# Fused attention and LoRA feed-forward layer: token stores moved from SyncE's queue to ScalarE's, and the order of two value products swapped in stage 1

## The chip, the cores and the metric

The kernel runs on one core of a Trainium2 chip. The metric is device time in microseconds of one execution. TensorE (PE) does matmuls and transposes, VectorE (DVE), ScalarE (ACT) and GpSimd (POOL) work on tiles in SBUF and PSUM, and SyncE (SP) issues most DMAs. Each engine runs its own instruction list strictly in order, and the lists meet at semaphores.

## The reference

Input x has 2 x 1024 tokens of 512 values. After a layernorm, two branches are computed on the same normalised tokens and added to x:

```python
xn = layernorm(x)
Q, K, V = heads(xn @ wq.T + bq), heads(xn @ wk.T + bk), heads(xn @ wv.T + bv)   # 16 heads of 32
Q, K = elu(Q) + 1, elu(K) + 1
KV = sum over tokens of K^T V;  K_sum = sum over tokens of K
att = (Q @ KV) / (Q . K_sum + 1e-8) @ wo.T + bo
scores = sigmoid(xn @ W_router); the best 2 of 8 experts by scores + expert_bias, weights w
gate = xn @ W_gate + shared LoRA + sum over experts of w * LoRA_e   (rank 8, scale 1/8)
up   = the same with W_up
ffn  = hidden @ W_down + LoRAs,  hidden = silu(gate) * up           (1376 wide)
out = x + att + ffn
```

## The kernel before, in words

All products are done as three matmuls on values split into a high part (fp32r) and the rest: high x high, high x low, low x high (`product`, L1216 to L1221). So each input needs a rounding on ScalarE (`round_to`, seen in the trace as L667) and a subtraction on VectorE (`sub`, seen as L865).

Stage 1 walks over 16 tiles of 128 tokens. Each engine has its own `stage1(t, half, s)`, called by `tiles` (L367): tiles 0 and 1 unrolled, 2 to 7 in a loop of pairs, 8 to 15 unrolled. s is the parity of t and picks one of two slots of most buffers. The order of the work is written out by hand in each list. For tile t, TensorE (L1260 to L1280) does:

1. K(t): keys, 12 matmuls of 512 columns into bank 1 (in the trace bank<-wk_h,xt and bank<-wk_l,xt);
2. T(t+1): four transposes of the next tile's normalised tokens xn (L1236);
3. on even tiles from 2 on, KV: 64 small matmuls that sum keys by values of the two tiles before (L1248);
4. Va(t): the first 384 value columns, 12 matmuls (128x384 in the trace), into ps_va;
5. Vz(t): the last 128 value columns with the 152 columns of LoRA and router, 12 matmuls (128x280), into ps_vz;
6. L(t-2): two transposes (L1257) of the LoRA values of tile t-2, weighted by their experts (the tile zst).

Tile 0 has T(1) between Va and Vz instead of behind K.

VectorE in tile t (L933 to L972): kb (L937, the keys plus bias, after K(t)), `compare(t-1)` of the router, the low part of the tokens of t+1 (`tokens_lo`, tile xt), `lora_weighted(t-2)` (L916 and L920, which write zst and release L(t-2)), layernorm statistics of t+2, `select(t-1)`, kf (L952), xn of t+2 (L878, after GpSimd's rstd), zraw (L960, a copy of Vz's last 152 columns), on even tiles `key_values` (L890), in tiles 8 to 11 the low part of a quarter of wq and in tiles 12 to 15 of wo, and `lora_lo(t-2)` (L929 and L930, tile zt, after ScalarE's high part).

ScalarE in tile t (L681 to L703): `tokens_hi(t+1)` (the high part of xt; it waits until the store of tile t-1, which used the same slot, has landed), krelu, kexp, the values of Va into vf (va_done), in tiles 8 to 15 a quarter of wq or wo (`WQ_PART`, `WO_PART`), then after zraw the values of Vz into vf (vf_done), rexp (L701), and `lora_out(t-2)` (the high part of zt, which waits for L(t-2)).

GpSimd computes rstd and the router's ranks and weights (`route`, L595). The split tokens xt of each tile go to the DRAM scratch scr_x by one DMA of 512 KB a tile, issued by SyncE (L430 to L432) behind the load of x for tile t+3 (L428); stage 2 (attention output) and stage 3 (feed-forward) read them back. Around these SyncE also issues stores of zt (L421), reads of scr_x (L411, L415) and the loads of down and up weights (L448, L445). After tile 0's store it issues some 3 MB of constants and weights (L437 to L442).

After tile 15 TensorE goes on with transposes of the summed keys by values (L1299) and the first queries, and from about a third of the span on the program is the feed-forward stage alone.

In the prediction and the rows, kb(t) is the instruction L937 of tile t, and K(t), T(t), Va(t), Vz(t), L(t), KV are the products above.

Of the kernel before, what the change touches and what calls it, by code (L numbers as in the profile page):

```python
# [19 lines left out]
ACT = mybir.ActivationFunctionType  # L20
F32 = mybir.dt.float32
F32R = mybir.dt.float32r

P = 128
BATCH, SEQ, D = 2, 1024, 512
TOK = BATCH * SEQ
KD = D // P
TILES = TOK // P
# [5 lines left out]
HEADS, DK = 16, 32  # L34
HC = P // DK
LO = DK // 2
E, R = 8, 8
# [4 lines left out]
NZ = 2 * ER + 2 * R + E  # L42
NV = D + NZ
VA = 3 * P
# [28 lines left out]
def program(nc, dram, out, scr_x, scr_z, scr_att, scr_w):  # L73
    ctx = ExitStack()
    with ctx:
        def sem(name):
            return ctx.enter_context(nc.semaphore(name))
# [20 lines left out]
        def at(name, shape, dt=F32):  # L98

            size = 4 * math.prod(shape[1:])  # L100
            t = nc.alloc_sbuf_tensor_at(name, shape, dt, offset=place[0])
            place[0] += -(-size // 32) * 32
            assert place[0] <= nc.sbuf_usable_end, (name, place[0])
            return t
# [57 lines left out]
        va_h = at("va_h", [P, KD, NV], F32R)  # L162
        va_l = at("va_l", [P, KD, NV], F32R)
# [3 lines left out]
        xt = at("xt", [P, 2, 2, KD, P], F32R)  # L167
# [9 lines left out]
        vf = at("vf", [P, 2, KD, HC, AUG])  # L177
# [16 lines left out]
        zraw = at("zraw", [P, 2, NZ])  # L194
        rexp = at("rexp", [P, E])
# [46 lines left out]
        ps_va, ps_vz = bank[4][:, 0:VA], bank[5][:, 0:P + NZ]  # L242
# [14 lines left out]
        wsetl_done = sem("wsetl_done")  # L257
# [6 lines left out]
        xtl_done = sem("xtl_done")  # L264
# [4 lines left out]
        va_ready = sem("va_ready")  # L269
        va_done = sem("va_done")  # L270
        vf_done = sem("vf_done")
        vz_ready = sem("vz_ready")
        zraw_done = sem("zraw_done")
        rexp_done = sem("rexp_done")
# [6 lines left out]
        scr_xd = [sem("scr_x_even"), sem("scr_x_odd")]  # L281
# [80 lines left out]
        def wait(eng, s, value):  # L362

            if not isinstance(value, int) or value > 0:
                eng.wait_ge(s, value)
# [11 lines left out]
        def behind(t, n):  # L377

            return not isinstance(t, int) or t >= n

        def ahead(t, n):

            return not isinstance(t, int) or t + n < TILES
# [11 lines left out]
        def _(sp):  # L395
            def load_x(t, s):
                sp.dma_start(xin[:, s, :], dram["x"][bass.ds(t * P, P), :]).then_inc(xin_in[s], 16)
# [16 lines left out]
            def x3_load(g):  # L414
                sp.dma_start(x3[:].rearrange("p t i k n -> p t (i k n)").bitcast(F32), scr_x[:, bass.ds(g * GT, GT)]  # L415
                             ).then_inc(x3_in, 16)
# [7 lines left out]
            def stage1(t, s, more=True):  # L424
                if more:

                    sp.wait_ge(ln_done, t + 2)
                    load_x(t + 3, 1 - s)  # L428

                sp.wait_ge(xtl_done, t + 1)  # L430
                sp.dma_start(scr_x[:, bass.ds(t, 1)], xt[:, s:s + 1].rearrange("p o i k n -> p o (i k n)").bitcast(F32)
                             ).then_inc(scr_xd[s], 16)  # L432

            stage1(0, 0)

            for dst, name in ((hmask, "headmask"), (hcol, "headcol"), (hrow_raw, "headrow"), (lomask, "lomask"), (bdn_raw, "b_dn"), (sb_dn, "sb_dn")):
# [49 lines left out]
            def x3r_load(t, s):  # L486
                sp.dma_start(x3r[:, s, :], dram["x"][bass.ds(t * P, P), :]).then_inc(x3r_in[s], 16)
# [20 lines left out]
            for j in range(2, GT):  # L508
                x3r_load(j, j)
            sp.wait_ge(q_ready, KD * 2)  # L510
            x3_load(2)
            sp.wait_ge(m_ready, BATCH * KD)
            for c in range(WO_CHUNK, X3_CHUNK):
# [151 lines left out]
        def _(act):  # L665
            def round_to(dst, src):
                return nc.scalar.activation(dst, src, ACT.Copy)  # L667
# [6 lines left out]
            def lora_out(t):  # L674
# [3 lines left out]
                round_to(zt4[:, :, 1], pst)  # L678
                round_to(zt4[0:ER, :, 0], pst[0:ER]).then_inc(zhi_done, 1)

            def stage1(t, half, s):  # L681
                first = isinstance(t, int) and t == 0
                if ahead(t, 1):
                    tokens_hi(t + 1, 1 - s, half + s)
                act.wait_ge(kb_done, t + 1)
                nc.scalar.activation(krelu[:], kb[:], ACT.Relu, scale=-1.0).then_inc(krelu_done, 1)
                act.wait_ge(krelu_done, t + 1)
                wait(act, kf_done, t)
                nc.scalar.activation(kexp[:], krelu[:], ACT.Exp, scale=-1.0).then_inc(kexp_done, 1)
                act.wait_ge(va_ready, t + 1)  # L690
                round_to(vf[:, s, 0:KD - 1, :, 0:DK], ps_va.rearrange("p (k h n) -> p k h n", h=HC, n=DK)).then_inc(va_done, 1)
                if isinstance(t, int) and t in WQ_PART:

                    act.wait_ge(s2_in, 16 * STAGE2_LOADS)
                    round_to(wq_h[:, WQ_PART[t]], w_raw[:, 1, WQ_PART[t]]).then_inc(wqh_done, 1)
                if isinstance(t, int) and t in WO_PART:
                    round_to(wo_h[:, WO_PART[t]], w_raw[:, 0, WO_PART[t]]).then_inc(woh_done, 1)

                act.wait_ge(zraw_done, t + 1)
                round_to(vf[:, s, KD - 1, :, 0:DK], ps_vz[:, 0:P].rearrange("p (h n) -> p h n", n=DK)).then_inc(vf_done, 1)  # L700
                nc.scalar.activation(rexp[:], zraw[:, s, NZ - E:], ACT.Exp, scale=-1.0).then_inc(rexp_done, 1)  # L701
                if behind(t, 2):
                    lora_out(t - 2)  # L703

# [510 lines left out]
        def _(pe):  # L1215
# [7 lines left out]
            def tile_of(dst, s, wh, wl, split_before=None):  # L1223

                for k in range(KD):
                    if split_before is not None:
                        pe.wait_ge(wsetl_done, split_before + k + 1)
                    last = product(dst, (xt_h[:, s, k, :], xt_l[:, s, k, :]), (wh[:, k, :], wl[:, k, :]),
                                   k == 0, k == KD - 1)
                return last  # L1230

            def transpose_tokens(t):
                pe.wait_ge(ln_done, t + 1)
                wait(pe, xtl_done, t)
                for k in range(KD):
                    last = nc.tensor.transpose(ps_xt[:, k * P:(k + 1) * P], xn[:, k * P:(k + 1) * P], ident[:])  # L1236
                last.then_inc(xt_ready, 1)

            def keys_by_values(t, pair, s):

                pe.wait_ge(kf_done, t + 1)
                pe.wait_ge(vf_done, t + 1)
                if s == 0:
                    pe.wait_ge(kvacc_done, pair + 1)
                for c in range(KD):
                    for h in range(HC):
                        col = c * P + h * DK
                        last = nc.tensor.matmul(ps_kv[h * DK:(h + 1) * DK, c * AUG:(c + 1) * AUG],  # L1248
                                                kf[:, s, col:col + DK], vf[:, s, c, h, :],
                                                start=(s == 0 and c == 0), stop=(s == 1), skip_group_check=True)  # L1250
                last.then_inc(kv_ready, 1)

            def lora_transposed(t):
                pe.wait_ge(zst_done, t + 1)
                wait(pe, zt_done, t)
                for k in range(2):
                    last = nc.tensor.transpose(ps_zt[:, k * P:(k + 1) * P], zst[:, k, :], ident[:])  # L1257
                last.then_inc(zt_ready, 1)

            def stage1(t, half, s):  # L1260
                first = isinstance(t, int) and t == 0
                pe.wait_ge(xtl_done, t + 1)
                wait(pe, kb_done, t)
                tile_of(ps_k[:], s, wk_h, wk_l, split_before=0 if first else None).then_inc(k_ready, 1)
                if ahead(t, 1) and not first:
                    transpose_tokens(t + 1)
                if s == 0 and behind(t, 2):
                    keys_by_values(t - 2, half - 1, 0)
                    keys_by_values(t - 1, half - 1, 1)
                wait(pe, va_done, t)  # L1270
                tile_of(ps_va, s, va_h[:, :, 0:VA], va_l[:, :, 0:VA], split_before=KD if first else None
                        ).then_inc(va_ready, 1)
                if first:
                    transpose_tokens(1)
                wait(pe, vf_done, t)
                if first:
                    pe.wait_ge(wsetl_done, 2 * KD + 1)
                tile_of(ps_vz, s, va_h[:, :, VA:], va_l[:, :, VA:]).then_inc(vz_ready, 1)
                if behind(t, 2):
                    lora_transposed(t - 2)  # L1280

            pe.sem_inc(u_ready, 1)
            pe.sem_inc(d_done, 1)
# [105 lines left out]
            kv_transposed(1)  # L1389
            queries(0, (3,))  # L1390
            pe.wait_ge(vf_done, TILES)
            pe.wait_ge(zraw_done, TILES)
            pe.wait_ge(zt_done, TILES - 1)
            m_of(0)
# [203 lines left out]
```

## Time and profile before

| What | us |
|---|---|
| Median of 3 runs | 674.25 (672.67 to 675.02) |
| Profiled execution, its time | 671.93 |
| Its span, first to last instruction | 670.1 |
| PE busy | 660.1 (99%) |
| DVE busy | 375.5 (56%) |
| ACT busy | 256.2 (38%) |
| POOL busy | 126.5 (19%) |

The granted TensorE clock is full over the whole span. Busy time is the union of an engine's instructions; the ends of matmuls are modelled and each overlaps the next, so the distance between the starts of two matmuls tells more of PE's pace than the duration of one. In the timeline each row has the start in us, the duration in us, the engine, the line, the operation, output<-input, and in brackets the time that the engine had been idle before it and what released it.

### The profile page before, as it was taken

How to read it: one execution, taken by the hardware profiler on the slowest of the kernel's cores; microseconds unless marked ns; L12 is line 12 of the kernel's file. 1: busy time of each engine (PE TensorE's matmuls, PEld its weight loads, DVE VectorE, ACT ScalarE, POOL GpSimd, SP SyncE). 2: the span in 40 equal slices, each digit the busy share in tenths (PEclk: the TensorE clock that was granted, in tenths of full speed). 3: DMA queues.
4: the chain of work that ended last, by engine and by line, in shares of the span. 5: the costliest groups of instructions: out<-in, count | busy, mean ns of one | idle time of the engine just before them, and what ended most of it. 6: DMA issues, size and time to landing. Idle time of an engine off the chain costs nothing.

```text
span 670.1 us, 10338 instructions
## 1 busy us (share of the span) xinstructions
PE 660.1 (99%) x3568; PEld 545.6 (81%) x3568; DVE 375.5 (56%) x697; ACT 256.2 (38%) x412; POOL 126.5 (19%) x290
## 2 busy tenths in 40 slices
PE   7999999999999999999999999999999999999998
PEld 6888999977777788888888888888888888888886
DVE  5577888778775956334345443445444326534433
ACT  4334454467235423323233333243233324323321
POOL 3466666636246230000000000000000000000000
PEclk9999999999999999999999999999999999999999
DMA  8856566754844679950025100011500001300001
GB/s 258 297 182 202 193 214 204 256 222 163 307 183 153 235 225 3 9 195 0 1 78 201 51 0 0 0 67 75 188 0 0 0 3 75 126 0 0 0 0 63
DMA packets 40778, 74.21 MB, mean 111 GB/s; under 512 B 19296, under 2 KB 20192, under 8 KB 38832
## 3 DMA queue, kind: packets, MB, share of 16 engines
q1 hardware_dynamic: 40400, 73.43, 39.0%
q0 software_dynamic: 208, 0.30, 0.4%
q8 instruction: 16, 0.26, 0.2%
q10 hardware_dynamic: 144, 0.13, 0.1%
q14 instruction: 10, 0.08, 0.0%
HBM read 52.81 MB, written 21.04 MB: 110 GB/s over the span
## 4 chain that ended last, share of the span: by engine, by line
PE 74%; POOL 9%; issue 6%; DVE 4%; DMA 2%; ACT 2%; POOLq 1%; SPq 0%; DVEq 0%; ACTq 0%
PE bank L1461 18%; PE bank L1219 15%; PE bank L1220 15%; PE bank L1221 15%; PE bank L1434 6%; DVE den L1065 2%; PE bank L1447 1%; PE bank L1445 1%; POOL vare L578 1%; POOL rstd L580 1%; POOL gt L605 1%; DMA scr_z<-zt 1%; POOL ssum L616 1%; DMA w_raw<-in_wkT 1%; POOL ssum L612 1%
## 5 line engine op out<-in xcount | busy, mean ns | idle before, releaser
L1219 PE MATMUL bank<-x,up_h 128*128 128x512 f32 (+1 forms) x352 | 137.1, 390 | 0.2 <-DVE x3r L1030 0.2
L1220 PE MATMUL bank<-x,up_h 128*128 128x512 f32 (+1 forms) x352 | 137.0, 389 | 0.0
L1221 PE MATMUL bank<-x,up_l 128*128 128x512 f32 (+1 forms) x352 | 136.9, 389 | 0.0
L1156 DVE TENSOR_TENSOR hf<-bank,silu 128x512 f32<-128x512 f32 x44 | 30.4, 692 | 154.5 <-issue 134.8
L1461 PE MATMUL bank<-dn,hid_h 128*128 128x512 f32 x352 | 108.8, 390 | 0.0
L667 ACT ACTIVATE hid_h<-hf 128x512 fp32r<-128x512 f32 x44 | 27.8, 633 | 142.5 <-DVE hf L1156 142.5
L1219 PEld LDWEIGHTS bank<-x,up_h 128*128 128x128 f32 x352 | 66.1, 188 | 14.4 <-issue 0.7
L1461 PEld LDWEIGHTS bank<-dn,hid_h 128*128 128x128 f32 x352 | 65.9, 188 | 14.5 <-DVE res L1181 0.6
L1221 PEld LDWEIGHTS bank<-x,up_l 128*128 128x128 f32 x352 | 66.1, 188 | 13.8
L1220 PEld LDWEIGHTS bank<-x,up_h 128*128 128x128 f32 x352 | 66.1, 188 | 13.6
L865 DVE TENSOR_TENSOR up_l<-up_raw,up_h 128x1024 fp32r<-128x1024 f32 x44 | 55.0, 1250 | 26.9 <-ACT up_h L667 26.9
L1461 PE MATMUL bank<-dn,hid_l 128*128 128x512 f32 x176 | 68.5, 389 | 0.0
L667 ACT ACTIVATE up_h<-up_raw 128x1536 fp32r (+1 forms) x44 | 64.6, 1474 | 1.7 <-DVE qf_odd L1023 1.7
L824 ACT ACTIVATE silu<-bank 128x512 f32<-128x512 f32 x44 | 26.3, 597 | 100.3 <-PE bank L1434 100.3
L1434 PE MATMUL bank<-z,up_h 128*128 128x512 f32 x176 | 54.2, 389 | 0.0
L865 DVE TENSOR_TENSOR hid_l<-hf,hid_h 128x512 fp32r<-128x512 f32 x44 | 30.5, 692 | 35.5 <-ACT hid_h L667 35.5
L667 ACT ACTIVATE dn<-dn_raw 128x576 fp32r (+1 forms) x44 | 30.1, 684 | 33.3 <-PE bank L1447 22.3
L1219 PE MATMUL bank<-va_h,xt 128*128 128x384 f32 (+1 forms) x128 | 41.9, 327 | 0.8 <-DVE va_l L865 0.8
L1221 PE MATMUL bank<-va_h,xt 128*128 128x384 f32 (+1 forms) x128 | 40.3, 315 | 0.0
L1220 PE MATMUL bank<-va_l,xt 128*128 128x384 f32 (+1 forms) x128 | 40.2, 314 | 0.0
L865 DVE TENSOR_TENSOR up_h<-up_raw,up_h 64x256 fp32r<-64x256 f32 x88 | 38.6, 439 | 0.6
L1461 PEld LDWEIGHTS bank<-dn,hid_l 128*128 128x128 f32 x176 | 33.0, 188 | 6.9
(166 smaller groups left out, 1081.0 us busy)
## 6 DMA issues: line engine op xcount, KB each, us to landing
x<-scr_x SPq DMA_DIRECT2D x7, 2048.0 KB, 7.5
up_raw<-in_ffn_up SPq DMA_DIRECT2D x11, 768.0 KB, 7.9
scr_x<-xt SPq DMA_DIRECT2D x16, 512.0 KB, 5.3
xin<-in_x SPq DMA_DIRECT2D x16, 256.0 KB, 4.5
scr_z<-zt SPq DMA_DIRECT2D x16, 256.0 KB, 2.0
x3r<-in_x SPq DMA_DIRECT2D x16, 256.0 KB, 3.6
scr_att<-x3r SPq DMA_DIRECT2D x16, 256.0 KB, 2.2
z<-scr_z SPq DMA_DIRECT2D x4, 1024.0 KB, 5.0
```

The source lines that it names most:

```text
L578: nc.gpsimd.tensor_tensor(vare[:], mv[:, 1:2], epsln[:], ALU.add).then_inc(vare_done, 1)
L580: nc.gpsimd.tensor_tensor(rstd[:], vare[:], mhalf[:], ALU.pow).then_inc(ln_rstd, 1)
L667: return nc.scalar.activation(dst, src, ACT.Copy)
L824: nc.scalar.activation(silu[:], ps_g[:], ACT.Silu).then_inc(silu_done, 1)
L865: return nc.vector.tensor_tensor(dst, a, b.bitcast(F32), ALU.subtract)
L1065: nc.vector.reciprocal(den[:], den[:]).then_inc(rden_done, 1)
L1156: nc.vector.tensor_tensor(hf[:], ps_u[:], silu[:], ALU.mult).then_inc(h_done, 1)
L1219: nc.tensor.matmul(dst, lh, rh, start=start, stop=False, **kw)
L1220: nc.tensor.matmul(dst, lh, rl, start=False, stop=False, **kw)
L1221: return nc.tensor.matmul(dst, ll, rh, start=False, stop=stop, **kw)
L1434: last = nc.tensor.matmul(dst[:], up_h[:, s, col:col + P], z4[:, :, a * 2 + b, :], start=False, stop=(b == 1))
L1461: d = nc.tensor.matmul(ps_out[j][:], h[:, s, cols], w[:, s, 0:DNB - 1], start=(first and i == 0), stop=False, skip_group_check=True)
```

## The change

Token stores: SyncE no longer issues them. ScalarE issues the store of tile t+1 in its tile t behind kexp, after a wait for the low part of the tokens of t+1; in tile 0 it issues those of tile 0 and 1. SyncE waits for all 16 stores before it reads back the third group of tokens.

Order in tiles 1 to 15: TensorE does Vz(t), then L(t-2), then Va(t). ScalarE evacuates Vz and does rexp first, then the part of wq or wo, then the values of Va, then `lora_out(t-2)`. Tile 0 keeps its order. VectorE's and GpSimd's lists are unchanged. KV waits for va_done of both tiles, since it is now the later one.

```diff
 # SyncE, stage1
-                sp.wait_ge(xtl_done, t + 1)
-                sp.dma_start(scr_x[:, bass.ds(t, 1)], xt[:, s:s + 1]...).then_inc(scr_xd[s], 16)
 # SyncE, stage 2
             sp.wait_ge(q_ready, KD * 2)
+            for s in range(2):
+                sp.wait_ge(scr_xd[s], 16 * TILES // 2)
             x3_load(2)
 # ScalarE
+            def store_tokens(t, s):
+                act.wait_ge(xtl_done, t + 1)
+                act.dma_start(scr_x[:, bass.ds(t, 1)], xt[:, s:s + 1]...).then_inc(scr_xd[s], 16)
 # ScalarE, stage1, behind kexp
-                act.wait_ge(va_ready, t + 1)
-                round_to(vf[:, s, 0:KD - 1, :, 0:DK], ps_va...).then_inc(va_done, 1)
+                if first:
+                    store_tokens(0, 0)
+                if ahead(t, 1):
+                    store_tokens(t + 1, 1 - s)
+                def values_out():
+                    act.wait_ge(va_ready, t + 1)
+                    round_to(vf[:, s, 0:KD - 1, :, 0:DK], ps_va...).then_inc(va_done, 1)
+                if first:
+                    values_out()
+                act.wait_ge(zraw_done, t + 1)
+                round_to(vf[:, s, KD - 1, :, 0:DK], ps_vz[:, 0:P]...).then_inc(vf_done, 1)
+                nc.scalar.activation(rexp[:], zraw[:, s, NZ - E:], ACT.Exp, scale=-1.0).then_inc(rexp_done, 1)
                 if isinstance(t, int) and t in WQ_PART:
                     act.wait_ge(s2_in, 16 * STAGE2_LOADS)
                     round_to(wq_h[:, WQ_PART[t]], w_raw[:, 1, WQ_PART[t]]).then_inc(wqh_done, 1)
                 if isinstance(t, int) and t in WO_PART:
                     round_to(wo_h[:, WO_PART[t]], w_raw[:, 0, WO_PART[t]]).then_inc(woh_done, 1)
-                act.wait_ge(zraw_done, t + 1)
-                round_to(vf[:, s, KD - 1, :, 0:DK], ...).then_inc(vf_done, 1)
-                nc.scalar.activation(rexp[:], ...).then_inc(rexp_done, 1)
+                if not first:
+                    values_out()
                 if behind(t, 2):
                     lora_out(t - 2)
 # TensorE, keys_by_values
                 pe.wait_ge(vf_done, t + 1)
+                pe.wait_ge(va_done, t + 1)
 # TensorE, stage1: values_a() is Va(t); values_z() is Vz(t), then L(t-2)
+                if first:
+                    values_a()
                     transpose_tokens(1)
+                    values_z()
+                else:
+                    values_z()
+                    values_a()
 # TensorE, ahead of m_of(0)
             pe.wait_ge(vf_done, TILES)
+            pe.wait_ge(va_done, TILES)
```

## Rows read from the trace of the kernel before

**Rows 1.** Busy time by stretch: us, then each engine's busy us, PEclk, DMA.

```profile
32.00:34.00 2.00, 1.18 (x8) 0.87 (x7) 1.90 (x9) 1.55 (x4) 0.00 (x0) 1.00 0.09 35
...
60.00:80.00 20.00, 20.00 (x231) 18.50 (x218) 15.56 (x52) 8.82 (x21) 11.65 (x39) 1.00 0.62 202
...
140.00:160.00 20.00, 19.36 (x92) 14.64 (x92) 15.98 (x25) 14.94 (x29) 4.54 (x5) 1.00 0.42 160
```

**Rows 2.** Timeline of PE, tile 7 into tile 8, from T(8) to T(9).

```profile
67.17 0.60 PE L1236 MATMUL bank<-ident_sb,xn 128*128 128x128 f32 x4
...
67.53 0.42 PE L1219 MATMUL bank<-va_h,xt 128*128 128x384 f32 x1
...
69.71 0.29 PE L1219 MATMUL bank<-va_h,xt 128*128 128x280 f32 x1
...
71.25 0.38 PE L1257 MATMUL bank<-ident_sb,zst 128*128 128x128 f32 x2
71.39 0.48 PE L1219 MATMUL bank<-wk_h,xt 128*128 128x512 f32 x1
...
74.28 0.60 PE L1236 MATMUL bank<-ident_sb,xn 128*128 128x128 f32 x4
```

**Rows 3.** Timeline of DVE, tile 7 and the start of tile 8.

```profile
68.22 0.69 DVE L937 TENSOR_TENSOR kb<-bank,bk_b 128x512 f32<-128x512 f32 x1
...
70.38 0.35 DVE L920 TENSOR_TENSOR zst<-zraw,wtok 128x64 f32<-128x64 f32 x2
...
73.39 0.31 DVE L960 COPY zraw<-bank 128x152 f32<-128x152 f32 x1
...
74.67 0.42 DVE L865 TENSOR_TENSOR zt<-bank,zt 64x256 fp32r<-64x256 f32 x1 [0.97 <-ACT zt L667]
...
75.62 0.69 DVE L937 TENSOR_TENSOR kb<-bank,bk_b 128x512 f32<-128x512 f32 x1
```

**Rows 4.** Timeline of ACT, tile 7 behind zraw.

```profile
73.74 0.28 ACT L667 ACTIVATE vf<-bank 128x128 f32<-128x128 f32 x1 [3.11 <-DVE zraw L960]
...
74.01 0.63 ACT L667 ACTIVATE zt<-bank 128x256 fp32r<-128x256 f32 x2
```

**Rows 5.** Timeline of DVE and ACT, tile 9 (with a part of wq).

```profile
83.25 0.69 DVE L937 TENSOR_TENSOR kb<-bank,bk_b 128x512 f32<-128x512 f32 x1
...
85.18 0.47 ACT L667 ACTIVATE vf<-bank 128x384 f32<-128x384 f32 x1
...
85.55 0.62 ACT L667 ACTIVATE wq_h<-w_raw 128x512 fp32r<-128x512 f32 x1
...
90.66 0.69 DVE L937 TENSOR_TENSOR kb<-bank,bk_b 128x512 f32<-128x512 f32 x1
```

**Rows 6.** Timeline of PE and DVE, tile 2: T(3), kb(2), L(0).

```profile
27.21 0.60 PE L1236 MATMUL bank<-ident_sb,xn 128*128 128x128 f32 x4
27.51 0.69 DVE L937 TENSOR_TENSOR kb<-bank,bk_b 128x512 f32<-128x512 f32 x1 [1.84 <-PE bank L1221]
...
33.16 0.44 PE L1257 MATMUL bank<-ident_sb,zst 128*128 128x128 f32 x2 [0.82 <-DVE zst L920]
```

**Rows 7.** ACT around the stores of tiles 0 and 1, and ScalarE's one DMA.

```profile
17.23 0.63 ACT L689 ACTIVATE kexp<-krelu 128x512 f32<-128x512 f32 x1
...
20.98 0.60 ACT L667 ACTIVATE xt<-bank 128x512 fp32r<-128x512 f32 x1 [0.29 <-PE bank L1236]
...
667.86 0.38 ACTq L389 DMA_DIRECT2D out<-res  x1
```

**Rows 8.** DMA issues of the page: KB each, median us to landing.

```profile
scr_x<-xt SPq DMA_DIRECT2D x16, 512.0 KB, 5.3
```

**Rows 9.** Waits over the span, us in total, times, longest us.

```profile
ACT xt L667 <- DMA scr_x<-xt: 13.4, 5, 5.3
```

**Rows 10.** Timeline, tile 15: kb(15), and PE's first transposes behind stage 1.

```profile
128.20 0.69 DVE L937 TENSOR_TENSOR kb<-bank,bk_b 128x512 f32<-128x512 f32 x1
...
131.43 0.60 PE L1299 MATMUL bank<-ident_sb,kvm 128*128 128x128 f32 x4
```

More of the change, by code:

```diff
@@ L428, in stage1 @@
                     load_x(t + 3, 1 - s)
-                sp.wait_ge(xtl_done, t + 1)
-                sp.dma_start(scr_x[:, bass.ds(t, 1)], xt[:, s:s + 1].rearrange("p o i k n -> p o (i k n)").bitcast(F32)
-                             ).then_inc(scr_xd[s], 16)
             stage1(0, 0)
@@ L679, in lora_out @@
                 round_to(zt4[0:ER, :, 0], pst[0:ER]).then_inc(zhi_done, 1)
+            def store_tokens(t, s):
+                act.wait_ge(xtl_done, t + 1)
+                act.dma_start(scr_x[:, bass.ds(t, 1)], xt[:, s:s + 1].rearrange("p o i k n -> p o (i k n)").bitcast(F32)
+                              ).then_inc(scr_xd[s], 16)
             def stage1(t, half, s):
@@ L689, in stage1 @@
                 nc.scalar.activation(kexp[:], krelu[:], ACT.Exp, scale=-1.0).then_inc(kexp_done, 1)
-                act.wait_ge(va_ready, t + 1)
-                round_to(vf[:, s, 0:KD - 1, :, 0:DK], ps_va.rearrange("p (k h n) -> p k h n", h=HC, n=DK)).then_inc(va_done, 1)
+                if first:
[4 more added lines that the diff above has]
+                    act.wait_ge(va_ready, t + 1)
+                    round_to(vf[:, s, 0:KD - 1, :, 0:DK], ps_va.rearrange("p (k h n) -> p k h n", h=HC, n=DK)).then_inc(va_done, 1)
+                if first:
+                    values_out()
+                act.wait_ge(zraw_done, t + 1)
+                round_to(vf[:, s, KD - 1, :, 0:DK], ps_vz[:, 0:P].rearrange("p (h n) -> p h n", n=DK)).then_inc(vf_done, 1)
+                nc.scalar.activation(rexp[:], zraw[:, s, NZ - E:], ACT.Exp, scale=-1.0).then_inc(rexp_done, 1)
                 if isinstance(t, int) and t in WQ_PART:
@@ L697, in stage1 @@
                     round_to(wo_h[:, WO_PART[t]], w_raw[:, 0, WO_PART[t]]).then_inc(woh_done, 1)
-                act.wait_ge(zraw_done, t + 1)
-                round_to(vf[:, s, KD - 1, :, 0:DK], ps_vz[:, 0:P].rearrange("p (h n) -> p h n", n=DK)).then_inc(vf_done, 1)
-                nc.scalar.activation(rexp[:], zraw[:, s, NZ - E:], ACT.Exp, scale=-1.0).then_inc(rexp_done, 1)
+                if not first:
+                    values_out()
                 if behind(t, 2):
@@ L1269, in stage1, with values_a, values_z @@
                     keys_by_values(t - 1, half - 1, 1)
-                wait(pe, va_done, t)
-                tile_of(ps_va, s, va_h[:, :, 0:VA], va_l[:, :, 0:VA], split_before=KD if first else None
-                        ).then_inc(va_ready, 1)
+                def values_a():
+                    wait(pe, va_done, t)
+                    tile_of(ps_va, s, va_h[:, :, 0:VA], va_l[:, :, 0:VA], split_before=KD if first else None
+                            ).then_inc(va_ready, 1)
+                def values_z():
+                    wait(pe, vf_done, t)
+                    if first:
+                        pe.wait_ge(wsetl_done, 2 * KD + 1)
+                    tile_of(ps_vz, s, va_h[:, :, VA:], va_l[:, :, VA:]).then_inc(vz_ready, 1)
+                    if behind(t, 2):
+                        lora_transposed(t - 2)
                 if first:
+                    values_a()
                     transpose_tokens(1)
[L1275 to L1280, printed above, removed]
+                    values_z()
+                else:
+                    values_z()
+                    values_a()
             pe.sem_inc(u_ready, 1)
```

## The prediction

> **What bounds the kernel now.** I read the busy time by stretch first: in stage 1 PE is busy 20.00 of 20 us while DVE has 15.56 and ACT 8.82 [rows 1]. PE's timeline says the same more sharply. T(8) to T(9) is 7.11 us with no idle bracket: T 0.36, Va 2.18, Vz 1.54, L 0.14, K 2.89 [rows 2]. So steady stage 1 is TensorE's stream and nothing in it waits. What waits is little: L(0) came 0.82 us late, for zst [rows 6], behind a token store that ScalarE waited 5.3 us for [rows 9]. Then I read DVE, which never waits for PE in this stretch: kb(7) to kb(8) is 7.40 us [rows 3], paced by its own list and by ACT's high part of zt, which it waited 0.97 us for. DVE is nearly as full a loop as PE, and that is what the change has to be read against.
>
> **What the early Vz can release: nothing.** Vz(7) starts at 69.71 and L(5) behind it at 71.25 [rows 2], but zraw(7) starts at 73.39 [rows 3], 2.1 us after. zraw is held by its place in DVE's list, which is unchanged. Making Vz end 2.18 us earlier brings zraw, rexp and the router not one step forward.
>
> **What the order adds on TensorE.** L(t-2) moves ahead of Va(t). It needs zst, which DVE finishes at kb(t) + 2.51: 68.22 to 70.38 + 0.35 [rows 3]. kb(t) itself waits for K(t): at T(3) 27.21 it started at 27.51, 0.30 later [rows 6]. So L can go no earlier than T + 0.30 + 2.51 + 0.04, where 0.04 is a handover (zraw's end 73.70, ACT's next at 73.74) [rows 3, 4]. That is T + 2.85. On odd tiles PE is there at T + 0.36 + 1.54 = T + 1.90, so it stands idle 0.95. On even tiles KV fills the gap. Before, Va lay between and hid it: L(5) at T + 4.08 was 0.5 behind zst's end at 70.73 [rows 2, 3]. The new loop of a tile is K end, kb, zst, L, Va, K: 0.30 + 2.51 + 0.04 + 0.14 + 2.18 + 2.89 = 8.06 us, odd or even. It closes on itself, so lateness isn't made up.
>
> **What the order adds on ScalarE.** Behind zraw stand vf of Vz, rexp and the high part of zt, at 73.74 and 74.01 [rows 4], and DVE waits for the last before kb(t+1). The change puts the values of Va in between: 0.37, the distance from that instruction to the next (85.18 to 85.55) [rows 5]. DVE's loop becomes 7.40 + 0.37 = 7.77, still under 8.06. In tiles 8 to 15 the part of wq or wo (0.62) also moves from the idle time ahead of zraw to behind rexp. I take 0.52 for it, its duration less the 0.10 by which the instruction ahead of it overlaps its start [rows 5]. DVE's low part of wq or wo waits for it too, but ends before zt's high part does. Loop: 7.41 (kb(9) to kb(10)) + 0.37 + 0.52 = 8.30 [rows 5], which is over 8.06 and so sets the pace there. Bounds: 8.06, if the part is hidden after all, and 7.41 + 0.47 + 0.62 = 8.50.
>
> **The stores.** SP loses 16 issues; nothing waits for them there but the loads behind. ScalarE gains 16 issues; its one such row is 0.38 us [rows 7]. From tile 1 on each lies behind kexp, in the idle time before vf, 3.11 us in tile 7 [rows 4]: nothing. Without that cover it would be 15 x 0.38 = 5.7. The waits for landed stores (13.4 us on ACT in all [rows 9]) go, since a store now starts some tile earlier than it is needed, but only the first ever reached PE. The start pays something: store 0 can't be issued before kexp(0) ends at 17.86, and lands by the median 5.3 [rows 7, 8] at 23.2, where ACT took xt(2) at 20.98. With 0.60 and about 0.69 for the two halves of xt, K(2) may start at 24.5; before, it started near 27.21 - 2.89 = 24.3 [rows 2, 6]. With kb and kf behind it I take 0.3. Bounds: 0, if it lands by 21, and 3.3, if it waits the 5.3 us that a store cost before [rows 9]: 5.3 less the 2.0 between xt(2)'s end and K(2). All of SP's constants and weights travel in that time. The Trainium skill ("DMA: Bandwidth & Descriptors", Queues, rings and completion order) says that each DMA engine goes round the queues that have work, a packet from each. By this rule a store on ScalarE's queue passes SP's backlog instead of standing in it, and the start costs the 0.3 or less; its section on issuing engines says that they share the same 16 engines, which speaks for more. No row of before has bulk on both queues.
>
> **Sum, as positions.** T(3) at 27.21 + 0.3 = 27.5. Six tiles at 8.06 put T(9) at 75.9; it was 74.28 [rows 2]. The stall of tile 2 is won and lost again in there. kb(8) is at 76.2, seven loops at 8.30 (tile 14 has head sums in place of statistics, taken as equal) put kb(15) at 134.3, against 128.20 [rows 10]: 6.1 late. Tile 15 has no tokens to round, so zst comes at kb + 2.51 - 0.60 (an estimate from the 0.6 that ACT's like instruction takes), then 0.04, L 0.14, Va 2.18: PE enters stage 2 at kb + 4.27 = 138.6, where it was 131.43 [rows 10], 7.1 late. DVE and ACT are only 6.1 late there, and PE had 0.64 idle in the stretch behind [rows 1], so some 0.6 comes back. The rest of the program is a full PE stream and moves by the same 6.5. From 671.93 of the profiled execution that is 678.4. The median of the runs is 2.3 above that execution, so the forecast is **680.7**.
>
> By bounds: the second pace at 8.06 takes 1.7 off, at 8.50 adds 1.4; the start takes 0.3 off or adds 3.0; the return may be 0 or 1.5. That is 677.8 to 685.7, the ends hardly together.
>
> **Rivals.**
> - *Faster.* zst comes in time for the moved L. The point is T + 1.90 on odd tiles, and it needs kb or the router's steps on DVE 0.95 earlier than rows show. If so, PE keeps its stream. T(3) to T(9) took 47.07 us [rows 2, 6] where the six tiles from kb(9) to kb(15) took 44.95 [rows 5, 10]; those 2.1 go with the store's wait, the 0.64 of stage 2 with them, and it ends at 671.5. Against it: DVE's list is the same and kb can't precede K's end. Chance 0.06.
> - *No difference.* The waits exist but overlap: DVE's loop stays near 7.5, PE loses 0.3 or so on odd tiles only, about 2 us, which eats the 2.1 won at the start: 674.2. Chance 0.06.
> - *Late stores.* The forecast, and store 0 lands as late as store 1 did: 683.7. For it, the backlog of weights; against it, the queue of its own. Chance 0.08.
> - *The clock.* The granted clock is 1.00, the 2.4 GHz level, even where PE was busy 1.18 of 2.00 us [rows 1], so idle times of 1 us in 8 shouldn't move it. At 1.2 GHz each tile's 7.11 us of PE work would double: three tiles make 21 us, so about 702. Chance 0.02. The Trainium skill ("TensorE: Matmul & The Clock Gate", A second HAM failure mode) describes small idles between groups of matmuls that make the clock swing; so far the trace speaks against it here.
>
> **How the numbers follow.** The forecast has 0.78. About 0.3% (2 us) is what a measurement of this kernel can tell from no change. Slower: 0.78 + 0.08 + 0.02 = 0.88; same 0.06; faster 0.06. The range takes the forecast's bounds and the late stores, and leaves out the other three: 677.0 to 685.5.
>
> **What would show it.** Right: an idle bracket of about 0.9 at L1257 released by zst L920 on odd tiles, T to T near 8.1 in tiles 3 to 7; kb to kb near 8.3 in tiles 8 to 13 with DVE waiting 1 us and more for zt; kb released by PE in tiles 3 to 7; PE busy some 6 us less than its span grows to; no wait of ACT for scr_x beyond tile 2. The store step is wrong if xt(2) on ACT starts after 24. The whole is wrong if T to T over tiles 9 to 14 stays near 7.5: then zst doesn't hang on kb as I read it.

## The result and the profile after

The changed kernel takes 682.74 us (median of 5 runs, 682.11 to 684.03) against 673.47 us before. The ratio is 1.0137, interval 1.0123 to 1.0151: slower by 9.3 us. The profiled execution took 683.07 us, span 681.3.

The page's first part and the busy time by stretch show where: PE does the same work and is no longer full in stage 1 (from 60 to 80 us it was busy 20.00 of 20 us before, [rows 1], and 19.39 after).

```profile
PE 662.3 (97%) x3568; PEld 545.4 (80%) x3568; DVE 376.1 (55%) x697; ACT 255.6 (38%) x412; POOL 124.3 (18%) x290
...
40.00:60.00 20.00, 17.92 (x166) 16.05 (x166) 15.22 (x52) 7.75 (x19) 11.20 (x36) 1.00 0.63 192
60.00:80.00 20.00, 19.39 (x170) 17.15 (x169) 13.13 (x42) 7.33 (x21) 12.16 (x40) 1.00 0.67 223
...
100.00:120.00 20.00, 18.94 (x166) 16.77 (x166) 14.58 (x45) 8.59 (x23) 12.41 (x38) 1.00 0.53 186
```

The timeline of tile 7 answers to [rows 2] and [rows 3]: T(8), kb(7), zst, L(5), Va(7), then T(9).

```profile
71.90 0.60 PE L1248 MATMUL bank<-ident_sb,xn 128*128 128x128 f32 x4
72.10 0.69 DVE L949 TENSOR_TENSOR kb<-bank,bk_b 128x512 f32<-128x512 f32 x1
...
74.26 0.35 DVE L932 TENSOR_TENSOR zst<-zraw,wtok 128x64 f32<-128x64 f32 x2
...
74.66 0.44 PE L1270 MATMUL bank<-ident_sb,zst 128*128 128x128 f32 x2 [0.61 <-DVE zst L932]
74.86 0.42 PE L1231 MATMUL bank<-va_h,xt 128*128 128x384 f32 x1
...
79.83 0.60 PE L1248 MATMUL bank<-ident_sb,xn 128*128 128x128 f32 x4
80.03 0.69 DVE L949 TENSOR_TENSOR kb<-bank,bk_b 128x512 f32<-128x512 f32 x1 [0.20 <-PE bank L1233]
```

L now waits for zst, which VectorE finishes 2.51 us after kb (74.61). T to T is 7.93 us where it was 7.11, and kb(8) is released by PE, which never happened there before. The even tile in front of it, where KV fills the gap, hardly changed: T(7) to T(8) is 8.03 us where it was 7.99. Over a pair of tiles the pace went from 7.55 to 7.98 a tile. The idle bracket, 0.61, is smaller than the loss of 0.8, because the modelled end of the last matmul before it reaches into the gap.

The timeline of tile 9 answers to [rows 4, 5]. Behind zraw stand vf of Vz, the part of wq, the values of Va and zt:

```profile
88.34 0.69 DVE L949 TENSOR_TENSOR kb<-bank,bk_b 128x512 f32<-128x512 f32 x1
...
93.50 0.31 DVE L972 COPY zraw<-bank 128x152 f32<-128x152 f32 x1
93.84 0.28 ACT L665 ACTIVATE vf<-bank 128x128 f32<-128x128 f32 x1 [3.48 <-DVE zraw L972]
...
94.12 0.62 ACT L665 ACTIVATE wq_h<-w_raw 128x512 fp32r<-128x512 f32 x1
94.64 0.48 ACT L665 ACTIVATE vf<-bank 128x384 f32<-128x384 f32 x1
94.77 0.69 DVE L877 TENSOR_TENSOR wq_l<-w_raw,wq_h 128x512 fp32r<-128x512 f32 x1 [0.96 <-ACT wq_h L665]
95.01 0.64 ACT L665 ACTIVATE zt<-bank 128x256 fp32r<-128x256 f32 x2
95.68 0.42 DVE L877 TENSOR_TENSOR zt<-bank,zt 64x256 fp32r<-64x256 f32 x1 [0.21 <-ACT zt L665]
...
96.63 0.69 DVE L949 TENSOR_TENSOR kb<-bank,bk_b 128x512 f32<-128x512 f32 x1
```

The distances are 0.52 for the part and 0.37 for the values, and kb to kb is 8.29 where it was 7.41. VectorE's wait shows at the low part of wq (0.96) more than at zt.

**Where the 11.1 us between the two profiled executions lie**, from the starts of T, kb and the first transposes behind stage 1 in both timelines:

| Stretch | before | after | difference |
|---|---|---|---|
| start to T(1) | 15.45 | 17.32 | +1.87 |
| T(1) to T(3) | 11.76 | 12.75 | +0.99 |
| T(3) to T(5), tiles 2 and 3 | 16.88 | 17.83 | +0.95 |
| T(5) to T(9), tiles 4 to 7 | 30.19 | 31.93 | +1.74 |
| T(9) to T(15), tiles 8 to 13 | 45.30 | 49.42 | +4.12 |
| T(15) to L1299 (L1321 after) | 11.85 | 13.37 | +1.52 |
| from there to the end | 538.67 | 538.68 | 0.0 |

All that the change takes away before T(1) is the issue of store 0, at 13.96 in the kernel before, and nothing waits for that store there. Over all the experiments below T(1) starts between 15.70 and 18.64, the latest of them with store 0 on SyncE, so I put its 1.87 down to the single execution; 11.1 - 1.9 = 9.2 is then near the 9.3 of the medians.

### The profile page after: what moved, and what is told of

It is laid out like the page before. It is cut to its first block, busy times and chain, and to the rows that moved or that the text cites. A ratio compares the mean times of both kernels' runs of the same rounds, so it can differ in the third digit from the quotient of the medians.

```text
span 681.3 us, 10343 instructions
## 1 busy us (share of the span) xinstructions
PE 662.3 (97%) x3568; PEld 545.4 (80%) x3568; DVE 376.1 (55%) x697; ACT 255.6 (38%) x412; POOL 124.3 (18%) x290
## 4 chain that ended last, share of the span: by engine, by line
PE 77%; POOL 9%; issue 7%; DVE 4%; DMA 2%; ACT 1%; POOLq 1%; SPq 0%; DVEq 0%; ACTq 0%
PE bank L1484 17%; PE bank L1231 16%; PE bank L1232 16%; PE bank L1233 16%; PE bank L1457 6%; DMA w_raw<-in_wvT 2%; PE bank L1470 1%; PE bank L1468 1%; POOL vare L576 1%; POOL gt L603 1%; POOL rstd L578 1%; DVE den L1077 1%; POOL ssum L614 1%; POOL ssum L610 1%; POOL gt L601 1%
## 5 line engine op out<-in xcount | busy, mean ns | idle before, releaser
L1231 PE MATMUL bank<-va_h,xt 128*128 128x384 f32 (+1 forms) x128 | 43.2, 337 | 1.1 <-DVE va_l L877 1.1
L1233 PE MATMUL bank<-va_h,xt 128*128 128x384 f32 (+1 forms) x128 | 40.4, 316 | 0.0
```

The source lines that it names most:

```text
L1231: nc.tensor.matmul(dst, lh, rh, start=start, stop=False, **kw)
L1233: return nc.tensor.matmul(dst, ll, rh, start=False, stop=stop, **kw)
```

## The experiments

Each was run beside the kernel before, in 5 to 12 executions, and its ratio is to the kernel before of the same rounds. Pace means T to T or kb to kb, from the timeline.

**Order alone and stores alone.**

```diff
 # e1_order_alone: the changed kernel, SyncE's stage1 as before
+                sp.wait_ge(xtl_done, t + 1)
+                sp.dma_start(scr_x[:, bass.ds(t, 1)], ...)
 # ScalarE
-                if first:
-                    store_tokens(0, 0)
-                if ahead(t, 1):
-                    store_tokens(t + 1, 1 - s)
 # e2_stores_alone: the kernel before, with store_tokens behind kexp on ScalarE, none on SyncE
```

> Edit: the stores are issued by SyncE again, the new order of TensorE and ScalarE stays. Theory (two loops, one over TensorE's wait for zst, one over ScalarE's work behind zraw, make the slowdown): 682 to 685 us, ratio to before 1.012 to 1.017; the start is about 1 us cheaper than after, ScalarE's waits for landed stores on even tiles come back and may add some tenths a tile. Rival (stores on ScalarE's queue cost most of it): 673 to 676.

> Edit: the kernel before, with only the token stores moved to ScalarE. Theory: T(3) about 1 us later than before for store 0, ScalarE's other waits for landed stores gone, TensorE's stream else unchanged: 672.5 to 675, ratio 0.998 to 1.002. Rival (the stores cost): 679 or more, kb to kb over 7.6 in tiles 8 to 13.

Measured: order alone 684.43 us, ratio 1.0155 (1.0137 to 1.0173); stores alone 672.95 us, ratio 0.9987 (0.9978 to 0.9996). The slowdown is the order's. In order alone the pace was 7.98 in tiles 5 and 6 and 8.28 in tiles 9 to 12, as after; the tenths that I had feared from the landed stores on even tiles didn't come, since the longer tile gives them time. Its start was dearer than after, not cheaper: ScalarE waited 5.39 us for store 1 and L(0) came 3.34 us late, because in this order L(0) stands ahead of Va(2) with nothing to hide behind. Behind this idle time the granted clock was at 0.50, the 1.2 GHz level, from 34.25 to 40.75, and T(3) to T(4) took 14.27 us (9.05 after). A stretch of it:

```profile
36.00:40.00 4.00, 4.00 (x13) 3.90 (x13) 1.30 (x4) 0.89 (x4) 3.01 (x10) 0.50 0.02 4
```

6.5 us at the half level are some 3.3 us of PE's work lost, an estimate. Only this execution of order alone has a trace. It is the slowest of five, with a mean granted clock of 0.993; the fastest, 682.83, has 1.000. So part of the difference between order alone and the changed kernel can be the clock's.

**Which loop costs what.** Four kernels put back one piece or two of the order.

```diff
 # e3_L_behind_Va: the changed kernel, TensorE
                 else:
                     values_z()          # without lora_transposed
                     values_a()
+                if behind(t, 2):
+                    lora_transposed(t - 2)
 # e4_parts_early: the changed kernel, ScalarE: the WQ_PART and WO_PART blocks ahead of
 #   act.wait_ge(zraw_done, t + 1)
 # e5_parts_and_zt_early: as e4, and
-                if not first:
-                    values_out()
                 if behind(t, 2):
                     lora_out(t - 2)
+                if not first:
+                    values_out()
 # e6_L_behind_Va_ACT_short: e3 and e5 together
```

> Edit: the changed kernel with L(t-2) behind Va(t) again, Vz(t) still first, ScalarE's new order kept. Theory: TensorE's wait for zst at L is gone, but DVE's loop over ScalarE stays: kb to kb 7.8 in tiles 4 to 7 (8.0 in the changed kernel), 8.3 in tiles 8 to 13 as in the changed kernel, TensorE's idle time moves to K(t) or KV; 680 to 682, ratio 1.009 to 1.013. Rival (the place of L is the whole cost): 673 to 675.

> Edit: the changed kernel with ScalarE's part of wq or wo ahead of the wait for zraw, as before. Theory: DVE's loop is 7.8 and TensorE's loop over zst, 8.0, sets the pace in all tiles: T to T 8.0 in tiles 9 to 14 (8.28 in the changed kernel), 6 to 7 tiles x 0.28 = 1.8 us off: 680.5 to 681.5. Rival (only DVE's loop counts, the wait for zst is a symptom): pace 7.8, 679.

> Edit: as e4, and the high part of zt ahead of the values of Va. ScalarE's order behind zraw is then as short as before, L(t-2) is still ahead of Va(t). Theory: TensorE's loop over zst stays, pace 8.0 as in e4, 680 to 681.5, idle brackets at L on odd tiles. Rival (ScalarE's order is the whole cost): 673 to 675.

> Edit: the changed kernel with L(t-2) behind Va(t) and ScalarE's part of wq or wo ahead of the wait for zraw, the high part of zt ahead of the values of Va; only the swap of Va and Vz and the stores stay. Theory: both loops are back at 7.4 or less, TensorE streams, T to T 7.55 in tiles 9 to 14: as e2, 672.5 to 675. Rival (the swap of Va and Vz itself costs): 678 or more.

| Kernel | us | ratio to before | pace, tiles 5 and 6 | pace, tiles 9 to 12 |
|---|---|---|---|---|
| after | 682.74 | 1.0137 (1.0123 to 1.0151) | 7.98 | 8.28 |
| L behind Va | 679.83 | 1.0097 (1.0079 to 1.0115) | 7.82 | 8.30 |
| parts early | 680.52 | 1.0123 (1.0101 to 1.0145) | 7.98 | 7.97 |
| parts and zt early | 680.14 | 1.0104 (1.0087 to 1.0121) | 7.98 | 7.98 |
| all three | 673.06 | 1.0013 (0.9986 to 1.0040) | 7.54 | 7.55 |

(Paces of T in all but L behind Va, where they are of kb.) The ratios are the ones to compare: the kernel before had a median of 673.59 beside the first and the last of the four experiments and of 672.77 beside the other two. Each loop alone holds the kernel at 680, and only without both is TensorE's stream back at the 7.55 of before. The medians hide two of the eleven executions of the last kernel, which took 679.97 and 680.38 us with mean granted clocks of 0.995 and 0.990; the other nine lie between 671.71 and 673.55. These two have no trace, and what held them stays open. With ScalarE's list as short as before, PE still waits for zst and still releases kb. PE and DVE in the kernel with parts and zt early, from T(10) to T(11) and kb(10):

```profile
87.42 0.60 PE L1248 MATMUL bank<-ident_sb,xn 128*128 128x128 f32 x4
87.62 0.69 DVE L949 TENSOR_TENSOR kb<-bank,bk_b 128x512 f32<-128x512 f32 x1 [0.61 <-PE bank L1233]
...
90.18 0.44 PE L1270 MATMUL bank<-ident_sb,zst 128*128 128x128 f32 x2 [0.61 <-DVE zst L932]
...
95.34 0.60 PE L1248 MATMUL bank<-ident_sb,xn 128*128 128x128 f32 x4
95.55 0.69 DVE L949 TENSOR_TENSOR kb<-bank,bk_b 128x512 f32<-128x512 f32 x1 [0.56 <-PE bank L1233]
```

With L behind Va, kb(10) stands 2.68 us behind T(11), far from K's end; that loop runs over VectorE and ScalarE, without PE:

```profile
91.74 0.60 PE L1248 MATMUL bank<-ident_sb,xn 128*128 128x128 f32 x4
...
94.42 0.69 DVE L949 TENSOR_TENSOR kb<-bank,bk_b 128x512 f32<-128x512 f32 x1
```

**TensorE's loop, shortened from another side.** If it runs over zst, an earlier zst must shorten it by as much.

```diff
 # e12_zst_early: as parts and zt early; VectorE, stage1
+                if behind(t, 2):
+                    lora_weighted(t - 2, s)
                 if ahead(t, 1):
                     tokens_lo(t + 1, 1 - s)
-                if behind(t, 2):
-                    lora_weighted(t - 2, s)
```

> Edit: as e5 (the changed order on TensorE, ScalarE's list as short as before), and VectorE weights the LoRA values of t-2 before it takes the low part of the tokens of t+1, so zst is ready some 0.6 us earlier. Theory (TensorE's loop runs over kb, zst, L, Va, K): the loop falls from 7.97 to about 7.4, which only odd tiles (7.11 of TensorE's own work) still feel; two tiles take 15.3 to 15.5 us against 15.94 in e5 and 15.10 before, the idle time at L on odd tiles falls from 0.6 to 0.2 or less: 675 to 677. Rival (something else than zst's place paces e5): 680.

Measured: 675.68 us, ratio 1.0035 (1.0022 to 1.0048). T(7) to T(9) took 15.31 us and T(9) to T(11) 15.29, where the kernel it was made from has 15.97 and 15.90, and from tile 4 to tile 14 no bracket stands at L any more. T(9), L(7) in tile 9 and T(11):

```profile
76.58 0.60 PE L1248 MATMUL bank<-ident_sb,xn 128*128 128x128 f32 x4
...
86.70 0.44 PE L1270 MATMUL bank<-ident_sb,zst 128*128 128x128 f32 x2
...
91.87 0.60 PE L1248 MATMUL bank<-ident_sb,xn 128*128 128x128 f32 x4
```

Shortened by some 0.6, the loop of 7.98 should be 7.4, over the 7.11 of TensorE's own work on odd tiles and under its 7.99 on even ones: odd tiles took 7.3 us and even ones 7.98. The loop over zst is shown by its size, not only by its presence.

**The start.** Store 0 back on SyncE, in the old order and in the new.

```diff
 # e7_store0_on_SP (from stores alone), e8_after_store0_on_SP (from the changed kernel)
 # SyncE
             stage1(0, 0)
+            sp.wait_ge(xtl_done, 1)
+            sp.dma_start(scr_x[:, 0:1], xt[:, 0:1]...).then_inc(scr_xd[0], 16)
 # ScalarE, behind kexp
-                if first:
-                    store_tokens(0, 0)
```

> Edit: as e2 (old order, stores on ScalarE), but store 0 is issued by SyncE where it was before. Theory: K(2) isn't late any more, the wait of 5.3 us for store 1 on SyncE's queue is gone, so T(3) to T(4) falls from 9.0 towards 8.0: 671.5 to 673, ratio 0.996 to 0.999. Rival (store 1 lands as late on its own queue, the weights take the bandwidth): as before, 673 to 674.

> Edit: the changed kernel, but store 0 is issued by SyncE where it was before. Theory: ACT takes xt(2) without a wait for the store, K(2) not 0.8 late, 0.8 to 1.5 us off the changed kernel: 681 to 682. Rival (the start's delay is hidden behind L(0)'s wait): 682.7.

Both missed. In the old order 673.15 us, ratio 1.0002 (0.9992 to 1.0013): nothing won. In the new order 684.30 us, ratio 1.0174 (1.0150 to 1.0197), no better than after and probably worse, since the two intervals barely touch. The rival of the first had the number, 673 to 674, but not the cause, for store 1 wasn't late: it landed 6.7 us after its issue. The rival of the second, 682.7, missed too. The wait for store 0 did go, and T(1) to T(3) in the new order fell from 12.75 to 11.79. But VectorE's statistics of tile 4 then waited for x, 3.10 us in the first and 2.51 in the second. Timeline of DVE and PE in the first of the two:

```profile
35.02 0.69 DVE L877 BATCH_NORM_STATS2 stats<-xin 128x6 f32<-128x512 f32 x1 [3.10 <-DMA xin<-in_x]
...
37.90 0.66 PE L1244 MATMUL bank<-ident_sb,xn 128*128 128x128 f32 x4 [0.64 <-DVE xn L886]
```

In the new order this delay went on into PE: L(1) came 2.75 us late, and behind that idle time the granted clock was at 0.50 from 42.75 to 45.75. A stretch of it:

```profile
43.00:45.00 2.00, 2.00 (x8) 2.00 (x7) 1.26 (x5) 0.00 (x0) 1.63 (x5) 0.50 0.85 264
```

In the kernel after, the wait for x is there too, 0.87, behind 3.14 for store 0 and 0.82 for L(0):

```profile
25.70 0.60 ACT L665 ACTIVATE xt<-bank 128x512 fp32r<-128x512 f32 x1 [3.14 <-DMA scr_x<-xt]
...
27.17 0.50 PE L1231 MATMUL bank<-wk_h,xt 128*128 128x512 f32 x1 [0.68 <-DVE xt L877]
...
30.79 0.60 ACT L665 ACTIVATE xt<-bank 128x512 fp32r<-128x512 f32 x1
...
33.96 0.44 PE L1270 MATMUL bank<-ident_sb,zst 128*128 128x128 f32 x2 [0.82 <-DVE zst L932]
...
34.77 0.69 DVE L881 BATCH_NORM_STATS2 stats<-xin 128x6 f32<-128x512 f32 x1 [0.87 <-DMA xin<-in_x]
```

xt(3) (30.79) has no wait for store 1, which in the kernel before cost 5.3 us there. In the first of the two experiments store 1, alone on ScalarE's queue, landed 6.7 us after its issue, where on SyncE's queue, behind 2 MB of wo and wq, it took 10.9: it passes the backlog. In the kernel after it stands behind store 0 and took 9.8 us, and it comes in time mostly because it is issued 2.3 us behind T(1) and not 5.0. The load of x for tile 4 stays behind the weights: issued at 21.96, landed near 34.7. It stood behind them in the kernel before as well, issued at 20.09 and landed 10.0 us later, but there VectorE was held until 32.05 by the wait for store 1 and found x ready. The next kernels test that.

```diff
 # e9 (from e7), e10 (from the kernel before), e11 (from e8): SyncE
-            sp.wait_ge(wsetl_done, 2 * KD)
-            sp.dma_start(w_raw[:, 0], dram["woT"]).then_inc(s2_in, 16)
-            sp.dma_start(w_raw[:, 1], dram["wqT"]).then_inc(s2_in, 16)
             ...
             stage1(1, 1)
+            sp.wait_ge(wsetl_done, 2 * KD)
+            sp.dma_start(w_raw[:, 0], dram["woT"]).then_inc(s2_in, 16)
+            sp.dma_start(w_raw[:, 1], dram["wqT"]).then_inc(s2_in, 16)
```

> Edit: as e7 (old order, stores on ScalarE, store 0 on SyncE), and SyncE issues its loads of wo and wq (1 MB each) behind the load of x for tile 4. Theory (the 2 MB of weights hold up whatever stands behind them on SyncE's queue: store 1 in the kernel before, x of tile 4 with the stores moved): DVE's wait for x of tile 4 (3.1 us in e7) is gone, T(3) to T(4) falls from 8.8 to 8.0 or less, T(4) to T(5) to 7.1 to 7.5; 1.3 to 2 us off before: 671 to 672, ratio 0.997 to 0.998. Rival (bandwidth, not order, holds them up): as e7, 673.

> Edit: the kernel before, with only the loads of wo and wq moved behind the load of x for tile 4 and store 1 on SyncE. Theory: store 1 lands by the 5 us of others, ScalarE's wait of 5.3 us before xt(3) is gone, as e9: 671 to 672, ratio 0.997 to 0.998; the queue that carries the stores makes no difference. Rival (ScalarE's queue is what frees store 1): 673.5, as before.

> Edit: the changed kernel, with store 0 on SyncE and the loads of wo and wq behind the load of x for tile 4. Theory: the whole start of the change's cost (T(1) to T(5), 30.6 us in the changed kernel against 28.6 before) goes, the loops stay at 7.97 and 8.29: 680.5 to 682. Rival (the start is noise of the single profile): 682.7 to 684.

Measured: 671.92 us, ratio 0.9975 (0.9965 to 0.9984); 671.12 us, ratio 0.9968 (0.9955 to 0.9980); 679.27 us, ratio 1.0089 (1.0076 to 1.0102), a little better than I had allowed. In the second, the old kernel with nothing but the weights moved, ScalarE takes xt(3) right behind its transposes, the statistics don't wait, and T(3) to T(4) is 8.01 us (9.03 before). The weights are issued only 0.5 us behind store 1, so the same bytes travel, yet store 1 landed 6.4 us after its issue (10.9 before) and x of tile 4 5.7 (10.0 before):

```profile
27.75 0.60 PE L1236 MATMUL bank<-ident_sb,xn 128*128 128x128 f32 x4
28.48 0.60 ACT L667 ACTIVATE xt<-bank 128x512 fp32r<-128x512 f32 x1 [1.87 <-PE bank L1236]
...
30.49 0.68 DVE L869 BATCH_NORM_STATS2 stats<-xin 128x6 f32<-128x512 f32 x1
...
35.76 0.60 PE L1236 MATMUL bank<-ident_sb,xn 128*128 128x128 f32 x4
```

With the weights out of the way it makes no clear difference which queue carries the stores (the two intervals overlap), and both versions beat both kernels. So it is the place in the queue that delayed the start; the bytes are the same, and the weights are only asked for from tile 8 on. And the order of the change alone, with a clean start on either side, costs 1.0089 - 0.9975 = 1.1%, or 7.7 us (7.4 by the medians). The stretches from T(5) on in the table above add up to the same, 1.74 + 4.12 + 1.52 = 7.4.

## Why the prediction was right, and where its sizes were off

**Direction and mechanism: right.** The range held the time, and both loops are there as built. Over the kernel before the forecast was +6.5 us and the measurement +9.3; against the forecast of 680.7 the time is only 2.0 off because the median before came out 0.8 lower this time, which is luck. The rival of late stores had 683.7, nearer to the time than the forecast, but not for its reason: store 0 cost 0.99 by T(3), not 3.3. Early Vz released nothing: zraw(7) starts at 77.27, 2.6 us after L(5), which stands behind Vz(7) (74.66), and with both loops undone the swap, together with the moved stores, measures 1.0013 (0.9986 to 1.0040).

**TensorE's loop, 8.06.** Measured 7.98. The handover from K's end to kb, taken as 0.30 from T(3), is 0.20 to 0.29 in steady tiles. The prediction wanted kb released by PE in all of tiles 3 to 7; the bracket stands only at even ones (kb(4), kb(6), kb(8)), though kb starts 0.20 behind T at the odd ones too. Six tiles took 49.76 us (30.07 to 79.83) where the sum had 48.4; the excess is in tiles 2 and 3, not in the loop.

**ScalarE's order, 8.30.** Measured 8.29, of it 0.37 and 0.52 as taken. kb(8) to kb(15) is 58.26 us against 58.1. Its wait shows at wq's low part, which I had called hidden; the length is the same.

**The start: undersized.** I gave it 0.3 by T(3), with 3.3 as upper bound, and had tile 2's stall won back. T(1) to T(3) grew by 0.99: store 0 was issued at 19.11 and landed near 25.7, 6.5 us, not the median 5.3, and K(2) began 4.94 us behind T(2) where it was 4.08. By the prediction's own sign, xt(2) on ScalarE after 24, this step failed: xt(2) started at 25.70, or at 23.8 if the late T(1) is taken off, where the sum had 23.2. Tiles 2 and 3 then took 17.83, not 16.1. The step that failed is "nothing waits for them there but the loads behind": one of SyncE's loads was x of tile 4, which stood behind 2 MB of weights before and after, and with the wait for store 1 gone, VectorE met x instead, landing 12.8 us after its issue. That is one part of the 17.83; the waits for zst at L(0) and L(1), 0.82 and 1.47 us, are others that the sum hadn't charged there, and no run parts them. The 2.1 us that the faster rival hoped for at the start were real, but not by moving the store to another queue: they came with the weights moved (0.9968, or 2.2 us).

By the rule of the Trainium skill ("DMA: Bandwidth & Descriptors", Queues, rings and completion order) a store on its own queue interleaves with the backlog instead of standing in it. The traces agree for store 1 (6.7 us from issue to landing in the old order with store 0 on SyncE, 10.9 before). They don't give the price of store 0, which had nothing to pass when SyncE issued it ahead of the weights.

**The tail: right; its return: wrong.** kb(15) to stage 2 is 4.33 us (4.27 predicted):

```profile
138.29 0.69 DVE L949 TENSOR_TENSOR kb<-bank,bk_b 128x512 f32<-128x512 f32 x1
...
140.23 0.44 PE L1270 MATMUL bank<-ident_sb,zst 128*128 128x128 f32 x2 [1.01 <-DVE zst L932]
...
142.62 0.60 PE L1321 MATMUL bank<-ident_sb,kvm 128*128 128x128 f32 x4
```

The 0.6 that I had coming back in stage 2 did not: from the first transposes behind stage 1 to the end both executions take 538.7 us. PE's idle time there would then hang on chains that start with PE's own queries, and move along with PE. That is argued from the equal stretch; no run took it apart. Together: 0.7 to T(3), 1.7 in tiles 2 and 3, 0.6 not returned, less 0.3 in tiles 4 to 7, make 2.7 of the 2.8 us between the forecast of +6.5 and the +9.3 measured.

**Clock.** It stayed at 1.00 (2.4 GHz) through every stretch of the profiled execution, stretches with PE at 17.92 of 20 us among them. Idle times like those of the two loops, 0.6 to 1.0 us a tile, never moved it in any trace, so the rival of a swinging clock isn't what slowed stage 1. At the start it is less remote than the prediction had it: behind idle times of 3.34 and 2.75 us two experiments ran at 0.50 for some microseconds. The other four executions of the changed kernel have mean granted clocks of 0.997 and no trace.

## What to carry to other kernels

When an engine is full, look for what each of its steps hides before reordering them: here Va stood between K and L and covered the 2.8 us that VectorE's list takes from K's end to zst, which comes behind kb in that list, and moving an independent product ahead of a dependent one bought nothing because its consumer was held by its own engine's list. Write down the loop that each order closes (K, kb, zst, L, Va, K) and add it up; two different loops can each hold the kernel at nearly the same pace, and undoing one gave back only about a quarter of the cost (1.0137 to 1.0097 or 1.0104), undoing both nearly all of it (1.0013). Moving a DMA to another queue doesn't remove a backlog, it changes who stands behind it; move the bulk that isn't needed soon.

## What the hardware showed that I had not expected

A 256 KB load issued behind 2 MB on the same queue landed 12.8 us later (21.96 to 34.77), with 1.5 MB of stores on the other queue in that time, where the median for such loads is 5.1 us. The granted clock fell to 0.50 inside five stretches of the experiments, each time behind an idle time of PE: 3.34 and 2.75 us in tiles 2 and 3, and 1.89, 2.19 and 2.28 us ahead of tile 0's keys in three; in two others idle times of 2.16 and 2.28 us at that place left it at 1.00. And two queues that each carry part of the start left its length as it was, until the order within one of them was changed.
